# More filler matmuls in the first periods of a fused decoder layer, and its start-up loads issued without waits

## The reference, cut to what matters

```python
x = x + attn(layernorm(x), w_in, b_in, w_out, b_out)      # attn itself returns its input + its output
x = x + xattn(layernorm(x), ctx, ctx, wq, wk, wv, wo)     # window 32, RoPE on q and k
x = x + ffn(layernorm(x), up, gate, down, router, w_up_s, w_gate_s, w_down_s)
```

## Time and profile before

| | us |
|---|---|
| median of 3 runs | 756.81 |
| lowest, highest | 754.93, 757.00 |
| the profiled execution's own time | 756.81 |
| its span in the profile | 755.0 |
| TensorE busy | 725.4 (96%) |
| VectorE, ScalarE, GpSimd busy | 536.4, 529.9, 529.4 |

### The profile page before, as it was taken

The page is one execution under the profiler, slowest core; times in us unless marked ns, Lnnn a source line. Parts: engine busy times, 40 slices in busy tenths (PEclk is TensorE's granted clock), DMA queues, the critical chain, the costliest instruction groups (busy, mean ns, idle before and its releaser), DMA issues.

```text
span 755.0 us, 31343 instructions
## 1 busy us (share of the span) xinstructions
PE 725.4 (96%) x11709; PEld 584.4 (77%) x11709; DVE 536.4 (71%) x1398; ACT 529.9 (70%) x1943; POOL 529.4 (70%) x857
## 2 busy tenths in 40 slices
PE   7889999999999999999999999999999998898994
PEld 5677888888888888888888888888888887676663
DVE  3567777777777777787877777777777778565763
ACT  2367777777777777877777777777777776764552
POOL 4566677777777788777777777777777776455654
PEclk9999999999999999999999999999999999999997
DMA  7000111111110000000000000000000000307430
GB/s 243 8 10 9 31 38 37 39 38 37 39 38 18 17 25 17 18 24 24 26 24 17 25 17 17 17 17 17 17 17 10 10 10 10 99 9 256 128 105 20
DMA packets 24562, 29.84 MB, mean 40 GB/s; under 512 B 3416, under 2 KB 20700, under 8 KB 24416
## 3 DMA queue, kind: packets, MB, share of 16 engines
q1 hardware_dynamic: 21056, 20.03, 8.9%
q0 software_dynamic: 2784, 6.56, 2.5%
q10 hardware_dynamic: 576, 1.26, 0.5%
HBM read 16.82 MB, written 11.47 MB: 37 GB/s over the span
## 4 chain that ended last, share of the span: by engine, by line
PE 87%; ACT 3%; DMA 3%; issue 2%; DVE 2%; SPq 1%; POOL 1%; POOLq 0%; DVEq 0%; ACTq 0%
PE P L306 8%; PE P L321 8%; PE P L362 7%; PE P L296 7%; PE P L286 7%; PE P L348 5%; PE P L334 5%; PE P L221 5%; PE P L238 5%; PE P L253 4%; PE P L380 4%; PE P L427 4%; ACT PX L890 2%; PE P L261 2%; PE P L351 2%
## 5 line engine op out<-in xcount | busy, mean ns | idle before, releaser
L890 ACT ACTIVATE PX<-P,mx 128x128 f32<-128x128 f32 x512 | 184.1, 413 | 53.7 <-DVE mx L602 53.7
L1059 POOL TENSOR_TENSOR PX<-PX,mx 128x512 f32<-128x512 f32 x128 | 132.2, 1041 | 111.5 <-DVE mx L607 111.2
L890 ACT ACTIVATION_READ_ACCUMULATOR PX<-P,mx 128x1 f32 x512 | 129.7, 253 | 0.0
L541 DVE TENSOR_REDUCE nmf<-P 128x4 f32<-128x512 f32 x128 | 81.4, 678 | 11.8 <-PE P L221 11.8
L602 DVE TENSOR_REDUCE mx<-P 128x4 f32<-128x512 f32 x128 | 81.9, 682 | 10.7 <-PE P L321 10.7
L854 ACT ACTIVATE PS<-P 128x512 f32<-128x512 f32 x128 | 69.5, 611 | 22.6 <-PE P L242 22.6
L1054 POOL TENSOR_TENSOR rq<-rq,tq 128x1024 f32<-128x1024 f32 x32 | 75.5, 2359 | 4.9 <-DVE rq L566 4.9
L1049 POOL TENSOR_TENSOR rk<-rk,tk 128x1024 f32<-128x1024 f32 x32 | 76.0, 2373 | 1.7 <-DVE tk L566 0.6
L899 ACT ACTIVATE PT<-P 128x512 f32<-128x512 f32 x128 | 69.2, 595 | 8.3 <-PE P L334 8.3
L522 DVE SCALAR_TENSOR_TENSOR KM<-P,c 128x512 f32<-128x512 f32 x32 | 24.0, 750 | 65.3 <-ACT qT L841 65.3
L306 PE MATMUL P<-cT,wq 128*128 128x128 f32 x512 | 69.2, 285 | 0.4 <-ACT cT L874 0.4
(11 more groups left out here) (155 smaller groups left out, 1828.8 us busy)
## 6 DMA issues: line engine op xcount, KB each, us to landing
xrow<-z_xs SPq DMA_DIRECT2D x39, 136.0 KB, 2.2
ew<-in_ew SPq DMA_DIRECT2D x9, 384.0 KB, 4.0
z_xs<-c SPq DMA_DIRECT2D x8, 408.0 KB, 3.7
x<-in_x SPq DMA_DIRECT2D x32, 64.0 KB, 3.0
cxT<-in_ctxT SPq DMA_DIRECT2D x31, 64.0 KB, 1.9
z_xs<-c SPq DMA_DIRECT2D x8, 136.0 KB, 3.0
out<-yst,xrow POOLq DMA_INDIRECT x39, 2.5
wk<-in_wk SPq DMA_DIRECT2D x1, 512.0 KB, 6.7
```

The source lines that it names most:

```text
L541: dve.tensor_reduce(nmf[b % 2][:, 0, r, :], v3(bank(f"s{r}")), AX.X, ALU.max, negate=True).then_inc(S["v_bm"][r], 1)
L890: t = act.activation(PX[(4 * b + r) % 6][:, c, :], p[:, c * 128:c * 128 + 128], ACT.Exp, bias=m[:, 0, r, c:c + 1], scale=1.0, accum_out=m[ ...
L1059: pool.tensor_tensor(X[:, :, :], X[:, :, :], mx[b % 3][:, 2, r, :].rearrange("p (h a) -> p h a", a=1).to_broadcast([128, 4, 128]), ALU.mul ...
```

## The change

The table of fillers grows from three entries to twelve (95 matmuls to 241). The loads tab and cb change places and are issued ahead of ScalarE's first activation, and c2 is issued behind them on ScalarE's queue, no longer on SyncE's. SyncE issues all its start-up loads with no wait between them, wq ahead of cxT[2]. In SyncE's loop one line goes behind another; the two never have work in the same period (next_cx ends with period 31, next_r begins with period 37).

```diff
-WARM = {('a', 0): 36, ('nmt', 0): 37, ('oT', 1): 22}
+WARM = {('a', 0): 36, ('qkv', 0): 8, ('v1', 0): 17, ('s0', 0): 51, ('nmt', 0): 40, ('st0', 0): 9, ('oT', 0): 13,
+        ('ln', 0): 10, ('qO', 0): 8, ('ds0', 0): 10, ('oT', 1): 28, ('ln', 1): 11}
...
             act.dma_start(cxT[0][:, :], A["ctxT"][0]).then_inc(S["d_cx"][0], 16)
+            act.dma_start(cb[:, :], A["cb"]).then_inc(S["d_cb"], 16)
+            act.dma_start(tab[:, :, :, :].rearrange("p w e t -> p (w e t)"), A["tab"]).then_inc(S["d_tab"], 16)
+            act.dma_start(c2[:, :], A["c2"]).then_inc(S["d_c2"], 16)
             act.wait_ge(S["p_init"], 2)
             act.activation(warm[:, :], nhalf[:, :], ACT.Exp)
-            act.dma_start(tab[:, :, :, :].rearrange("p w e t -> p (w e t)"), A["tab"]).then_inc(S["d_tab"], 16)
-            act.dma_start(cb[:, :], A["cb"]).then_inc(S["d_cb"], 16)
...
-            sp.wait_ge(S["d_x"][0], 16)
             sp.dma_start(wvT[:, :, :].rearrange("p t n -> p (t n)"), A["wvT"]).then_inc(S["d_wv"], 16)
-            sp.wait_ge(S["d_wk"], 16)
+            sp.dma_start(wq[:, :, :, :].rearrange("p e c n -> p (e c n)"), A["wq"]).then_inc(S["d_wq"], 16)
             load_cx(2)
-            sp.dma_start(c2[:, :], A["c2"]).then_inc(S["d_c2"], 16)
-            sp.dma_start(wq[:, :, :, :].rearrange("p e c n -> p (e c n)"), A["wq"]).then_inc(S["d_wq"], 16)
-            sp.wait_ge(S["d_wv"], 16)
             sp.dma_start(woT[:, :, :].rearrange("p t n -> p (t n)"), A["woT"]).then_inc(S["d_wo"], 16)
...
                 tile(next_r, "xl", s - 37, 2)
+                tile(next_r, "xl", s - 37, 3)
                 batch(next_cx, s - 4)
-                tile(next_r, "xl", s - 37, 3)
```

## The result

| | kernel before | changed kernel |
|---|---|---|
| median of 6 runs, us | 756.90 | 761.27 |
| lowest, highest | 754.93, 758.62 | 759.99, 762.94 |
| ratio to before, 95% interval | | 1.0057 [1.0042, 1.0074] |
| the profiled execution's own time | 756.81 | 765.12 |
| its span | 755.0 | 763.0 |

The change costs 4.3 us (3.2 to 5.6). The forecast was 1.55 us more, 758.4; the range ended at 761.0. So the sign of the sum was right and its size was not, and "slower by over 0.3%" had been given only 0.28.

The account below looks back on a forecast made before the run. TensorE, full in the middle, was taken as the bound, so start-up delays reach the end. Terms 2.30 - 1.07 = 1.23, plus 0.08 and 0.24, gave + 1.55 us on 756.81: 758.4 us, range 756.0 to 761.0.

Parts of the forecast that it names:

- slower by over 0.3%: Outcome class for the whole kernel's time, beginning at 759.1 us; given a chance of 0.28.
- The 51 fillers: Ahead of b_s(0) in the start-up: nothing covers them, they take 3.09 us, and b_s starts 2.30 us later.
- the 1.07 us given back by the upper clock: From b_s to b_nm(0): 5.11 us at the upper clock instead of 6.18, giving back 1.07.
- since it lies just where c2 would now be moved, I take the lower half, 0.3 us: Start-up loads: moving c2 delays wvT by 0.3 us, to 11.9, between bounds of nothing and 1.1 us.
- the hole at 9.0 to 10.5 us: Low DMA rate in the start-up, holding some 0.3 MB, expected to soften c2's delay of wvT.
- the rule of the Trainium skill that I had set beside the sum: DMA engines alternate between queues by packet, so c2 takes turns from wvT; the sum up to 0.8 us more.
- The 13 ahead of b_oT(0) fill their pause (0.79): Start-up fillers ahead of b_oT(0): they fit their pause of 0.79 us, so no term was added.
- 4.4 us of work without a pause, rise at 10.7: TensorE's start-up clock: it rises after 4.4 us of unbroken work, at about 10.7 us.
- The late-clock rival: Clock rises only among the 51 fillers: b_s at 19.4, + 4.9, 761.7 us; 759.1 to 762, chance 0.17.
- The ten fillers ahead of d_s(0): On the chain ahead of d_s(0): they take 0.60 us over a pause of 0.36, + 0.24.
- ln(1): Fillers ahead of ln(1): called covered, with no cost in the sum.
- slower: transfers: Start-up: c2's full 1.1 us, or ScalarE's first tile up to 1 us late; 759.1 to 760, chance 0.10.

Follow-up runs that it names:

- e13: The kernel before with SyncE's three start-up waits taken out and c2 left on its queue; ratio 0.9995 [0.9977, 1.0012].
- e14: The kernel before with cb and tab issued ahead of ScalarE's first activation, cb first; ratio 1.0002 [0.9986, 1.0018].
- e12: The kernel before with c2 issued on ScalarE's queue behind cb instead of on SyncE's; ratio 1.0041 [1.0022, 1.0060].
- e11: The kernel before with the 13 fillers ahead of b_oT(0) alone added; one execution with its trace, 768.18 us.
- e7: The changed kernel again, unchanged, on another chip with a second trace; 767.15 against 764.81 us, ratio 1.0036 [1.0018, 1.0055].
- e3: The kernel before with the new table of fillers alone, its loads kept; 760.75 us, ratio 1.0018 [1.0002, 1.0035].
- e6: The kernel before with only the 51 fillers ahead of b_s(0) added; ratio 1.0055 [1.0030, 1.0079].
- e9: The kernel before with 8 fillers added ahead of a_qkv(0) and loads ordered by need; 764.88 against 765.65 us, ratio 0.9979.
- e1: The changed kernel without the 51 fillers ahead of b_s(0); 759.97 against 758.80 us for the kernel before, ratio 1.0021.
- e2: The kernel before with every edit but the filler table's; 759.70 us, ratio 1.0022 [1.0006, 1.0039].
- e5: The kernel before with 8 fillers added ahead of a_qkv(0) and 8 ahead of c_v(0, 1); ratio 0.9985 [0.9968, 1.0003].

## Why the prediction was right in part and wrong in size

**Right.** The middle is full and hands the start-up's delay on unchanged (2.59 at 62 us, 1.98 at 640). The 51 fillers were the largest term: KM was ready at 12.33, nothing covered them, and they took 3.01 us where 3.09 were reckoned. b_nm came 5.07 us after b_s (5.11 reckoned; 6.1 before), so the 1.07 us given back by the upper clock are confirmed. Removing SyncE's waits brought nothing (e13). ScalarE's changed order cost nothing (e14); the table load took 1.28 us again and ended by 4.4. The six more fillers ahead of b_oT(1) cost nothing, and so did the swapped line.

**The loads, too small a value taken.** The step "since it lies just where c2 would now be moved, I take the lower half, 0.3 us" failed. wvT landed at 12.51 instead of 11.57, +0.94 us, near the upper bound of 1.1; e12 alone shows it at 12.90. I had counted the hole at 9.0 to 10.5 us as room for c2. But a hole late in wvT's flight doesn't give back what c2 took from wvT before it. The measured bandwidth of the changed kernel, in slices of 0.5 us from 0 (compare), shows the hole filled and the transfer done no sooner:

```profile
GB/s 0 0 0 61 190 358 335 354 317 333 294 331 349 313 336 370 353 411 419 400 436 409 395 428 420 395 418 336 205 92 74 45 6 0 0 0 0 0 0 0
```

The traffic of the two queues says where c2 took its turns (q1 is SyncE's queue, q10 ScalarE's; packets, MB, share), first from 7.5 to 9.0 us before:

```profile
q1 hardware_dynamic: 243, 0.48, 82.4%
q10 hardware_dynamic: 51, 0.11, 18.6%
```

and in the changed kernel:

```profile
q10 hardware_dynamic: 148, 0.41, 71.2%
q1 hardware_dynamic: 155, 0.16, 29.9%
```

Ahead of the hole ScalarE's queue moved 0.30 MB more and SyncE's 0.32 MB less. In the hole itself, from 9.0 to 10.5 us, it was SyncE's queue that moved more, 0.51 MB instead of 0.21: most of what filled it was that queue's own data. e12, with c2 moved and nothing else, has the same 0.41 and 0.16 MB from 7.5 to 9.0. c2's own time from issue to landing went from 3.9 to 9.4 us, so most of it passed beside wvT:

```profile
wvT<-in_wvT SPq DMA_DIRECT2D x1, 512.0 KB, 9.4
c<-in_c ACTq DMA_DIRECT2D x1, 356.0 KB, 9.4
```

By the rule of the Trainium skill that I had set beside the sum (DMA: Bandwidth & Descriptors, section Queues, rings and completion order: each engine takes turns between the queues, packet by packet) up to 0.8 us more than my sum was to be expected; the trace agrees, with 0.65 (c_v at 12.65, not 12.0). The weight should have been on that end.

**Fillers ahead of b_oT(0), a cover that wasn't one.** "The 13 ahead of b_oT(0) fill their pause (0.79)" failed. The pause ended with ScalarE's oT, but the bank that the fillers write to came free, with VectorE's vpad, only 0.11 us before that, so the fillers began when the pause was nearly over. They cost 0.60 us, the same in the changed kernel (delay from 1.83 to 2.43) and alone (e11). To see it one had to ask of each filler group not only how long the pause is but who holds its bank.

**The clock, a rule read from one event.** "4.4 us of work without a pause, rise at 10.7" was wrong: it rose at 4.3 us in the first trace and at 9.7 in e7. Even the one event was read a little early: the granted clock of the kernel before rose at 16.5 us, not 16.1. For the time it mattered little, because wvT was waited for anyway. b_s started at 16.52 where 16.04 was forecast: 0.65 for wvT, less 0.17 by which c_v and the 51 took a little less than reckoned. The late-clock rival (b_s at 17.04 for a rise at 13.0, 19.4 for one later still) did come true in e3, at 17.81 with a rise at 15.0.

**Small terms.** The ten fillers ahead of d_s(0) were given 0.24 and cost nothing in the first trace; the delay grew by 0.16 from 28 to 62 us (2.43 to 2.59), where nothing but the d_s term was forecast. A part of that is ln(1), called covered, whose 11 fillers began 0.20 us late behind VectorE's nmf:

```profile
52.47 0.79 PE L200 MATMUL P<-ones 128*128 128x128 bf16 x11 [0.20 <-DVE nmf L542]
```

The 0.28 us outside the span were in no term.

**The sum again.** 2.6 from the trace and 0.28 outside it make 2.9 us, where 1.55 were forecast: + 0.60 for wvT (the delay at 20 us is 1.83, forecast 1.23), + 0.60 for b_oT(0), + 0.28 outside, less 0.16 for the small terms (- 0.08, - 0.24, + 0.16). The third chip's 2.8 (1.4 to 4.2) is this. The first chip's 4.3 (3.2 to 5.6) is 1.4 more, 0.3 at the least; that rest is not explained. The range was drawn too narrow above for a sum whose three larger errors all point one way. The rival "slower: transfers" priced one mechanism alone and ended at 760, and no case added a cover that fails.

## What to carry to other kernels

A filler stands ahead of its stage's waits, so it is free only if the pause is longer than the filler and the filler may start when the pause does: check who frees the buffer that it writes to, and when. Fillers that follow work with no pause behind them are paid in full, however good they are for the clock (e6: 3.5 us paid, 1.0 got back). A load that nobody needs soon belongs behind the urgent ones on their own queue, not beside them on another one (e12, e9). And of a change of a few tenths of a per cent, one trace's start-up tells which steps moved, not what the time will be: take two traces of each kernel, and leave out what both kernels do in some executions.

## What the runs showed of the hardware that I had not expected

- The granted clock of one and the same kernel rose at 4.3 us in one execution and at 9.7 in another (changed kernel), at 16.5 and 16.6 in two of the kernel before; in e1, e2, e3, e5, e6, e11 and e12 it rose within the first 36 fillers (3.6 to 4.7 us), fell at 7.0 to 8.1, after a pause of 1.3 to 1.8 us behind them, and rose again at 10.5 to 17.3.
- Where no clock record stands yet, the granted clock of the profile reads 1.00 although the fillers of 0.112 us and a c_v of 2.04 run at the lower level. Before the first rise only durations tell the clock.
- c2 on ScalarE's queue goes with 0.28 us more outside the span in all seven kernels that have it there.
- When ScalarE's queue gets more to do, SyncE's gets less, though the sum stays: from 7.5 to 9.0 us 0.41 and 0.16 MB instead of 0.11 and 0.48.
- Near 680 us ScalarE waits 2.4 to 3.8 us for something that the profile calls "remote", in the traces of two chips always, in those of a third never, whichever the kernel, and TensorE's clock falls to the lower level behind it (granted clock 0.83 and 0.66 over 680 to 690 us in the two traces shown). In e1 and e3 there is no such wait, and the clock falls at 697 and 701 us instead. What "remote" stands for is open.
